# Back state of a three-step gated recurrence turned through DRAM instead of by TensorE, with the queues of all engines reordered around its hand-over

## The chip, the cores and the metric

The program runs on one core of a Trainium2 chip. The metric is device time in microseconds of one execution. It is bound to float32 accuracy, so every operand of a product is split into a high part and a low part (fp32r), and each product is three matmuls: high by high, high by low, low by high.

## The reference

For 32 graphs of 256 nodes with 256 features (`x`, shape 32 x 256 x 256, one shared `adj` of 256 x 256), four layers follow each other, each as `x = layernorm(x + layer(x))`:

```python
# layer 0: gated recurrence, 3 steps (both message directions use adj, so the two halves of w3, w4, w5 are summed)
for _ in range(3):
    a  = adj @ h
    z  = sigmoid(a @ W3 + h @ U3 + b)      # update gate
    r  = sigmoid(a @ W4 + h @ U3 + b)      # reset gate
    hv = tanh(a @ W5 + (r * h) @ U5 + b)
    h  = (1 - z) * h + z * hv
# layer 1: rel = adj.T * ((x Wq) @ (x Wk).T); rel = rel / row norm; out = rel @ (x Wv)
# layer 2: out = (adj @ x) @ W + b
# layer 3: out = norm_adj @ (x @ W) + b
```

## The kernel before

Two graphs form a pair; there are 16 pairs, and LAST is 15. The state of a pair is held in two forms. `feat` has features on the partitions and 512 nodes (two graphs) along the free axis; the products with U3 and with the reset state need it. `node` has nodes on the partitions; the product with adj (`mix`) needs it. After each step the new state comes out as `feat`, so it has to be turned to get `node`.

Two lanes work side by side, each with its own PSUM banks. The front lane does steps 0 and 1 of pair p; the back lane does step 2 of pair p-1 and then the other three layers (`main`) of that pair. At the end of step 1 the front lane writes the new state into the back lane's state (`hand_over_h`).

One step is, for each half k of the output features: `mix` (adj by node, 12 matmuls of 256 columns), `base` (U3 by feat), `reset`, `update`, `candidate_mixed` (a by W5) and `candidate_reset` (reset state by U5), each of the last five 6 matmuls of 512 columns. ScalarE (ACT) makes the high parts, the gates and tanh; VectorE (DVE) makes the low parts, the elementwise steps, the statistics of the layer norms, and the fills of PSUM with residual and bias; GpSimd (POOL) does the power -1/2 of the variances; SyncE (SP) issues the transfers.

Each engine runs its own instructions in a written order: `start()` (everything up to the first regular pair), `body(p, q)` in a loop over p = 2 to 14 with q = p - 1 (13 passes), and `finish()`. Every operation waits on semaphores by count and then does its work, so an operation that waits holds up everything behind it on its engine. The numbers of the loop body repeat with the period of one pass.

There were two ways to turn a state. The front state between step 0 and step 1 went through DRAM: VectorE transposes 32 x 32 blocks (`turn_state`, two instructions), SP writes them to a scratch tensor and reads them back with four transfers (`move_blocks`), ACT and VectorE split the result (`moved_hi`, `moved_lo`). The back state went through TensorE: `turn_h(state_b, ...)` issues four 128 x 128 transposes for each of two graphs into `front.ps1`, and `node_hi` and `node_lo` split from there. The next `mix(front, ...)` writes the same PSUM banks, so it waited for `state_b.s_node_lo`. In the loop the order on TensorE around it is: `mix_nodes(main, q, 1, 0..1)`, `convolve(main, q, 1, 0)`, the two `turn_h(state_b)`, `convolve(main, q, 1, 1)`, and in the next pass `mix(back)` twice, `mix(front)` twice, `base(back)` twice, `reset(back)`. There are 15 hand-overs: two in `start()`, 13 in the loop.

Of the kernel before, what the change touches and what calls it, by code (L numbers as in the profile page):

```python
# [21 lines left out]
P = 128  # L22
# [16 lines left out]
class State:  # L39


    def __init__(self, sb, sem, name, full, by_graph, by_blocks):
# [118 lines left out]
def build(nc, x, adj, w3_w, w3_b, u3_w, u3_b, w4_w, w4_b, w5_w, w5_b, u5_w, u5_b, wq, wk, wv,  # L161
          l2_w, l2_b, l3_w, l3_b, out):
    B, N, D = x.shape
# [12 lines left out]
    with ExitStack() as ctx:  # L176
# [43 lines left out]
        state_f = State(sb, sem, "hf", [P, C, T], [P, G, C, D], True)  # L220
        state_b = State(sb, sem, "hb", [P, C, T], [P, G, C, D], False)
# [14 lines left out]
        state_f.blocks, state_f.moved = quarters(front.gate), quarters(front.z)  # L236

# [6 lines left out]
        def nodes(name, dt=F32):  # L244
# [13 lines left out]
                      (nodes("v_hi", F32R), nodes("v_lo", F32R)), rel_split,  # L258
# [10 lines left out]
        main.sum_blocks, main.sum_moved = (t[:].rearrange("p g c d -> p (g c) d") for t in (main.normed, main.result))  # L269

# [56 lines left out]
        def _(sp):  # L327
# [72 lines left out]
            keep_input(0)  # L400
            with sp.Fori(1, LAST) as p:
# [4 lines left out]
                move_blocks(state_f, p)  # L406
                store(main, p - 1)
# [7 lines left out]
        def _(pool):  # L415
# [29 lines left out]
            def body(q):  # L445
# [3 lines left out]
                for k in range(2):  # L449
                    inverse_norm(main, q, k)  # L450
                for k in range(2):
                    inverse_std(main, q, 1, k)
# [5 lines left out]
            def finish():  # L458
# [7 lines left out]
                for k in range(2):  # L466
                    inverse_norm(last_pair, 0, k)
                inverse_std(last_pair, 0, 1, 0)
                inverse_norm(main, LAST - 1, 1)
                inverse_std(last_pair, 0, 1, 1)  # L470
                inverse_std(main, LAST - 1, 1, 1)
                inverse_std(main, LAST - 1, 2, 0)
                for k in range(2):
                    inverse_std(last_pair, 0, 2, k)
                inverse_std(main, LAST - 1, 2, 1)
                inverse_std(main, LAST - 1, 3, 0, True)
# [32 lines left out]
        def _(pe):  # L509
# [83 lines left out]
            def mix(L, n, k, pair=None, turned=False):  # L593
# [6 lines left out]
                if pair is not None and later(pair):  # L600
                    pe.wait_ge(state_b.s_node_lo, upto(pair - 1, k))
# [199 lines left out]
            def body(p, q):  # L801

                for k in range(2):
                    mix(back, q, k)
                for k in range(2):
                    mix(front, 2 * p, k, p)
                for k in range(2):
                    base(back, q, k)
                for k in range(2):
                    reset(back, q, k)  # L810
                candidate_mixed(back, q, 0)
                for k in range(2):
                    update(back, q, k)
                candidate_mixed(back, q, 1)
                for k in range(2):
                    candidate_reset(back, q, k)
                base(front, 2 * p, 0, p)
                reset(front, 2 * p, 0)
                base(front, 2 * p, 1, p)
                reset(front, 2 * p, 1)  # L820
                candidate_mixed(front, 2 * p, 1)
# [3 lines left out]
                update(front, 2 * p, 1)  # L825
                candidate_reset(front, 2 * p, 1)
                for k in range(2):
                    keys(main, q, k)
                values(main, q, 0)
                for k in range(2):  # L830
                    relate(main, q, k)
                base(front, 2 * p + 1, 0)
                values(main, q, 1)
                base(front, 2 * p + 1, 1)
                sum_squares(main, q, 0)
                attend(main, q, 0)
                sum_squares(main, q, 1)
                for k in range(2):
                    mix(front, 2 * p + 1, k)
                attend(main, q, 1)  # L840
                reset(front, 2 * p + 1, 0)
                candidate_mixed(front, 2 * p + 1, 0)
                reset(front, 2 * p + 1, 1)
                mix_nodes(main, q, 0, 0)
                update(front, 2 * p + 1, 0)
                mix_nodes(main, q, 0, 1)
                for k in range(2):
                    convolve(main, q, 0, k)
                candidate_reset(front, 2 * p + 1, 0)
                candidate_mixed(front, 2 * p + 1, 1)  # L850
                update(front, 2 * p + 1, 1)
# [3 lines left out]
                convolve(main, q, 1, 0)  # L855
                for k in range(2):
                    turn_h(state_b, p, k)
                convolve(main, q, 1, 1)

            def finish():  # L860

                mix(back, LAST - 1, 0)
                mix(front, 2 * LAST, 0, LAST)
                mix(back, LAST - 1, 1)
                mix(front, 2 * LAST, 1, LAST)
                for k in range(2):
                    base(back, LAST - 1, k)
                for k in range(2):
                    reset(back, LAST - 1, k)
                for k in range(2):  # L870
                    base(front, 2 * LAST, k, LAST)
                for k in range(2):
                    reset(front, 2 * LAST, k)
                candidate_mixed(front, 2 * LAST, 1)
                candidate_mixed(front, 2 * LAST, 0)
                update(front, 2 * LAST, 0)
                candidate_reset(front, 2 * LAST, 0)
                update(front, 2 * LAST, 1)
                candidate_reset(front, 2 * LAST, 1)
                update(back, LAST - 1, 0)  # L880
                candidate_mixed(back, LAST - 1, 0)
                for k in range(2):
                    turn_h(state_f, 2 * LAST + 1, k)
# [7 lines left out]
                candidate_reset(back, LAST - 1, 0)  # L891
                update(front, 2 * LAST + 1, 0)
                for k in range(2):
                    candidate_mixed(front, 2 * LAST + 1, k)
                candidate_reset(front, 2 * LAST + 1, 0)
                update(front, 2 * LAST + 1, 1)
                candidate_reset(front, 2 * LAST + 1, 1)
                candidate_mixed(back, LAST - 1, 1)
                candidate_reset(back, LAST - 1, 1)
                for k in range(2):  # L900
                    turn_h(state_f, 2 * LAST + 2, k)
                base(front, 2 * LAST + 2, 0)
# [7 lines left out]
                for k in range(2):  # L910
                    update(front, 2 * LAST + 2, k)
                candidate_mixed(front, 2 * LAST + 2, 0)
                candidate_reset(front, 2 * LAST + 2, 0)
                keys(main, LAST - 1, 0)
                candidate_mixed(front, 2 * LAST + 2, 1)
                candidate_reset(front, 2 * LAST + 2, 1)
                relate(main, LAST - 1, 0)
# [3 lines left out]
                values(main, LAST - 1, 0, True)  # L921
                keys(last_pair, 0, 0)
                relate(main, LAST - 1, 1)
                keys(last_pair, 0, 1)
                values(last_pair, 0, 0, True)
                for k in range(2):
                    relate(last_pair, 0, k)
                sum_squares(main, LAST - 1, 0)
# [1314 lines left out]
```

## Time and profile before

| | us |
|---|---|
| median of 3 runs | 1214.63 (1214.09 to 1214.99) |
| the profiled execution, its device time | 1214.77 |
| its span, first to last instruction | 1212.9 |
| TensorE busy in the span | 1198.3 |
| VectorE busy | 1002.6 |
| ScalarE busy | 655.7 |
| GpSimd busy | 191.7 |

The device time stands 1.9 us above the span: what lies before the first and after the last instruction. A matmul's duration in the trace is its latency; matmuls overlap, so what one costs TensorE is the distance from its start to the next start. Durations of other engines overlap their successor a little too. Starts are microseconds from the span's start.

### The profile page before, as it was taken

The numbers are of one execution on the slowest core, as the hardware profiler recorded it, in microseconds if no ns is written. First come the engines' busy times: TensorE is split into PE (matmuls) and PEld (weight loads), VectorE is DVE, ScalarE is ACT, GpSimd is POOL, SyncE is SP. The second block draws the span as 40 slices with busy tenths as digits, with TensorE's granted clock in tenths as the row PEclk, the third lists the DMA queues.
The fourth block names the chain that finished last, engine by engine and source line by source line (L and its number), as shares of the span: only waits on it lengthen the run. The fifth ranks groups of instructions, "written<-read, shape, count | busy, mean of one in ns | idle before, by whom it ended". The sixth has DMA issues, their size and how long they took to land.

```text
span 1212.9 us, 21243 instructions
## 1 busy us (share of the span) xinstructions
PE 1198.3 (99%) x7454; PEld 1079.2 (89%) x7454; DVE 1002.6 (83%) x2220; ACT 655.7 (54%) x1179; POOL 191.7 (16%) x447
## 2 busy tenths in 40 slices
PE   9999999999999999999999999999999999999997
PEld 8789899898988989899898998989889898998896
DVE  7689788897878879788897888978789797885898
ACT  5455555555555555555555555555555555554442
POOL 1002021110211203012020211102111030120022
PEclk9999999999999999999999999999999999999998
DMA  6030221303113030220302213031130302200001
GB/s 209 18 88 18 70 71 35 104 0 88 50 35 104 0 104 35 52 87 14 107 17 69 69 35 104 0 87 52 35 104 0 104 35 51 87 12 24 1 2 35
DMA packets 105021, 66.93 MB, mean 55 GB/s; under 512 B 65690, under 2 KB 98468, under 8 KB 104996
## 3 DMA queue, kind: packets, MB, share of 16 engines
q1 hardware_dynamic: 104784, 66.08, 18.2%
q0 software_dynamic: 192, 0.52, 0.2%
q8 instruction: 15, 0.25, 0.1%
q14 instruction: 10, 0.08, 0.0%
q10 hardware_dynamic: 20, 0.01, 0.0%
HBM read 35.13 MB, written 23.07 MB: 48 GB/s over the span
## 4 chain that ended last, share of the span: by engine, by line
PE 97%; DVE 2%; POOL 0%; ACT 0%; issue 0%; DVEq 0%; POOLq 0%
PE b_ps L520 41%; PE f_ps L520 32%; PE f_ps L515 15%; PE b_ps L515 7%; PE f_ps L682 1%; PE b_ps L746 1%; PE b_ps L564 0%; PE f_ps L1057 0%; DVE f_stats L1683 0%; DVE hf_feat L1699 0%; DVE f_gate L1699 0%; DVE b_rh_lo L1725 0%; PE b_ps L579 0%; DVE b_ps L1720 0%; PE f_ps L589 0%
## 5 line engine op out<-in xcount | busy, mean ns | idle before, releaser
L428 POOL TENSOR_TENSOR b_var_eps<-b_moments,eps 128x2 f32<-128x2 f32 x120 | 34.7, 289 | 904.2 <-DVE b_moments L1690 904.2
L1120 ACT ACTIVATE f_cand<-f_ps,bias_c 128x512 f32<-128x512 f32 x66 | 45.4, 689 | 85.2 <-PE f_ps L520 85.2
L430 POOL TENSOR_TENSOR b_rstd<-b_var_eps,neg_half 128x2 f32<-128x2 f32 x120 | 88.0, 733 | 9.4
L1068 ACT ACTIVATE b_rh_hi<-b_ps 128x512 fp32r<-128x512 f32 x90 | 53.6, 596 | 63.0 <-PE b_ps L520 62.9
L1108 ACT ACTIVATE f_gate<-f_ps,bias_r 128x512 f32<-128x512 f32 x66 | 45.3, 686 | 71.0 <-PE f_ps L520 71.0
L1068 ACT ACTIVATE b_a_hi<-normed 128x512 fp32r<-128x512 f32 x60 | 37.8, 630 | 60.0 <-DVE normed L1699 60.0
L520 PE MATMUL f_ps<-adjT_hi,hf_node_hi 128*128 128x256 f32 x264 | 66.4, 285 | 0.0
L520 PE MATMUL f_ps<-adjT_lo,hf_node_hi 128*128 128x256 f32 x264 | 65.0, 280 | 0.0
L1582 DVE TENSOR_TENSOR f_cand<-f_z,f_cand 128x512 f32<-128x512 f32 x66 | 45.4, 688 | 23.0 <-ACT f_cand L1120 22.9
L1725 DVE TENSOR_TENSOR b_rh_lo<-b_ps,b_rh_hi 128x512 fp32r<-128x512 f32 x90 | 61.1, 679 | 4.0 <-ACT b_rh_hi L1068 3.9
L1566 DVE TENSOR_TENSOR f_gate<-f_gate,hf_feat 128x512 f32<-128x512 f32 x66 | 44.7, 678 | 20.0 <-ACT f_gate L1108 20.0
L1068 ACT ACTIVATE f_a_hi<-f_ps 128x512 fp32r<-128x512 f32 x66 | 38.9, 591 | 38.3 <-PE f_ps L520 38.3
L1560 DVE TENSOR_TENSOR b_a_lo<-b_ps,b_a_hi 128x512 fp32r<-128x512 f32 x30 | 19.4, 686 | 48.6 <-ACT b_a_hi L1068 48.6
L1116 ACT ACTIVATE f_z<-f_ps,bias_z 128x512 f32<-128x512 f32 x66 | 45.0, 683 | 26.6 <-PE f_ps L515 26.5
L1560 DVE TENSOR_TENSOR f_a_lo<-f_ps,f_a_hi 128x512 fp32r<-128x512 f32 x66 | 44.9, 681 | 13.8 <-ACT f_a_hi L1068 13.6
L1187 ACT ACTIVATE result<-result,b_shift,b_rstd 128x256 f32<-128x256 f32 x56 | 30.6, 594 | 46.2 <-POOL b_shift L436 46.2
L520 PE MATMUL f_ps<-hf_feat_hi,u3T_hi 128*128 128x512 f32 x132 | 52.3, 396 | 0.2 <-DVE u3T_lo L1486 0.2
L1068 ACT ACTIVATE hf_feat_hi<-hf_feat 128x512 fp32r<-128x512 f32 x64 | 38.7, 627 | 25.1 <-DVE hf_feat L1646 22.3
L520 PE MATMUL f_ps<-f_a_hi,w4T_hi 128*128 128x512 f32 x132 | 51.9, 393 | 0.0
L520 PE MATMUL f_ps<-hf_feat_hi,u3T_lo 128*128 128x512 f32 x132 | 51.7, 391 | 0.0
L515 PE MATMUL f_ps<-f_a_lo,w34T_hi 128*128 128x512 f32 x132 | 51.5, 390 | 0.0
L520 PE MATMUL f_ps<-f_rh_hi,u5T_lo 128*128 128x512 f32 x132 | 51.5, 390 | 0.0
(340 smaller groups left out, 4304.4 us busy)
## 6 DMA issues: line engine op xcount, KB each, us to landing
x_front<-in_x SPq DMA_DIRECT2D x16, 512.0 KB, 3.9
x_blocks<-in_x SPq DMA_DIRECT2D x60, 128.0 KB, 2.9
input_t<-hf_feat SPq DMA_DIRECT2D x15, 512.0 KB, 3.0
turn_sum<-normed SPq DMA_DIRECT2D x14, 512.0 KB, 2.7
result<-turn_sum SPq DMA_DIRECT2D x56, 128.0 KB, 2.9
turn_f<-f_gate SPq DMA_DIRECT2D x14, 512.0 KB, 2.7
f_z<-turn_f SPq DMA_DIRECT2D x56, 128.0 KB, 2.8
out<-result SPq DMA_DIRECT2D x14, 512.0 KB, 3.2
```

The source lines that it names most:

```text
L428: pool.tensor_tensor(Y.var_eps[:, g], Y.moments[:, g, :, 1], eps[:], ALU.add).then_inc(Y.s_var, 1)
L430: pool.tensor_tensor(Y.rstd[:, g], Y.var_eps[:, g], neg_half[:], ALU.pow).then_inc(Y.s_rstd, 1)
L515: last = pe.matmul(bank, s, m, start=start and i == 0, stop=stop and i == len(terms) - 1, skip_group_check=True)
L520: return pe.matmul(bank, s, m, start=start, stop=stop, skip_group_check=True)
L1068: return act.activation(dst, src, ACT.Copy)
L1108: act.activation(L.gate[:, k], L.ps0[:, k], ACT.Sigmoid, bias=bias_r[:, k:k + 1]).then_inc(L.s_r, 1)
L1116: act.activation(L.z[:, k], L.ps0[:, k], ACT.Sigmoid, bias=bias_z[:, k:k + 1]).then_inc(L.s_z, 1)
L1120: act.activation(L.cand[:, k], L.ps1[:, k], ACT.Tanh, bias=bias_c[:, k:k + 1]).then_inc(L.s_tanh, 1)
L1560: dve.tensor_tensor(L.a_lo[:, k], L.ps1[:, k], full(L.a_hi[:, k]), ALU.subtract).then_inc(L.s_a_lo, 1)
L1566: dve.tensor_tensor(L.gate[:, k], L.gate[:, k], L.state.feat[:, k], ALU.mult).then_inc(L.s_rh, 1)
L1582: dve.tensor_tensor(L.cand[:, k], L.z[:, k], L.cand[:, k], ALU.mult).then_inc(L.s_zc, 1)
L1725: dve.tensor_tensor(lo[:, g], src, full(hi[:, g]), ALU.subtract).then_inc(done, 1)
```

## The change

The back state is turned the way the front state already was. `State` always has the semaphores of the block path; the back state gets a DRAM scratch, its blocks are written into the back lane's `kept` tile and read back into its `cand` tile. SP moves the back's blocks behind the front's in each pass, ahead of the store. All of `turn_h(state_b, ...)`, `node_hi(state_b, ...)` and `node_lo(state_b, ...)` go; two `turn_state`, two `moved_hi` and two `moved_lo` per pair come in. `mix(front, ...)` no longer waits for the back's `node_lo`, but for the tanh that last read its bank. The tiles of `x_hi`, `x_lo` and of the attention's `v_hi`, `v_lo` are swapped: v now shares the back lane's `a` tiles, x has its own. The order of all queues is written anew.

```diff
@@ set-up
+        state_b.scratch = scratch("turn_b")
+        state_b.blocks, state_b.moved = quarters(back.kept), quarters(back.cand)
...
-                      (nodes("v_hi", F32R), nodes("v_lo", F32R)), rel_split,
+                      (per_graph(back.a_hi), per_graph(back.a_lo)), rel_split,
...
+        main.x_hi, main.x_lo = nodes("x_hi", F32R), nodes("x_lo", F32R)
@@ SyncE
+            move_blocks(state_b, 1)
             with sp.Fori(1, LAST) as p:
...
                 move_blocks(state_f, p)
+                move_blocks(state_b, p + 1)
                 store(main, p - 1)
@@ TensorE, mix
-                if pair is not None and later(pair):
-                    pe.wait_ge(state_b.s_node_lo, upto(pair - 1, k))
+                if pair is not None:
+                    pe.wait_ge(front.s_tanh, upto(n - 1, k))
@@ TensorE, body, first operations (was: mix back x2, mix front x2, base back x2, reset back x2, ...)
                 for k in range(2):
+                    mix(front, 2 * p, k, p)
+                for k in range(2):
+                    base(back, q, k)
+                base(front, 2 * p, 0, p)
+                for k in range(2):
                     mix(back, q, k)
+                reset(front, 2 * p, 0)
...
@@ TensorE, body, last operations
                 for k in range(2):
                     mix_nodes(main, q, 1, k)
-                convolve(main, q, 1, 0)
-                for k in range(2):
-                    turn_h(state_b, p, k)
-                convolve(main, q, 1, 1)
+                for k in range(2):
+                    convolve(main, q, 1, k)
@@ ScalarE, body, first operations
                 for k in range(2):
+                    input_hi(p, k)
+                for k in range(2):
+                    moved_hi(state_b, q, k, q + 1)
+                for k in range(2):
+                    a_hi(front, 2 * p, k)
+                for k in range(2):
                     a_hi(back, q, k)
@@ VectorE, body, first operations
                 for k in range(2):
+                    turn_blocks(p, k)
+                for k in range(2):
+                    input_lo(p, k)
+                for k in range(2):
+                    moved_lo(state_b, q, k)
@@ VectorE, body, last operations
                 hand_over_h(p, 0)
+                keep(front, 2 * p + 1, 1)
                 conv_x_lo(main, q, 1, 1)
-                fill(main, q, 1, 0)
+                turn_state(state_b, p, 0)
                 candidate_part(front, 2 * p + 1, 1)
-                keep(front, 2 * p + 1, 1)
+                hand_over_h(p, 1)
                 conv_ax_lo(main, q, 1, 0)
-                hand_over_h(p, 1)
+                turn_state(state_b, p, 1)
                 fill(main, q, 1, 1)
                 conv_ax_lo(main, q, 1, 1)
...
@@ TensorE, start, around the first hand-over
-                base(back, 0, 0)
-                for k in range(2):
-                    turn_h(state_b, 0, k)
-                base(back, 0, 1)
+                for k in range(2):
+                    mix(front, 2, k, 1)
+                prepare(8)
+                candidate_mixed(front, 2, 1)
+                for k in range(2):
+                    base(back, 0, k)
                 for k in range(2):
                     mix(back, 0, k)
```

In `finish()` the last pair has no hand-over; its order changes as well, with the same operations.

## Rows read from the trace of the kernel before

**Rows 1.** The page: busy us of each engine, share of the span, instructions.

```profile
PE 1198.3 (99%) x7454; PEld 1079.2 (89%) x7454; DVE 1002.6 (83%) x2220; ACT 655.7 (54%) x1179; POOL 191.7 (16%) x447
```

**Rows 2.** The page: the chain that ended last, share of the span by engine.

```profile
PE 97%; DVE 2%; POOL 0%; ACT 0%; issue 0%; DVEq 0%; POOLq 0%
```

**Rows 3.** Waits of TensorE: waiter, what released it, us in total, times, longest.

```profile
PE b_ps L520 <- ACT hb_feat_hi L1068: 2.3, 2, 1.4
```

**Rows 4.** Windows (length, busy by engine, clock): start; 13 passes; finish; one pass; its end.

```profile
0.00:124.55 124.55, 120.25 (x707) 106.11 (x708) 97.97 (x200) 67.97 (x117) 14.46 (x35) 1.00 0.27 81
124.55:1082.47 957.92, 957.92 (x5983) 864.37 (x5981) 799.78 (x1768) 530.76 (x962) 154.71 (x364) 1.00 0.19 57
1082.47:1205.63 123.16, 120.13 (x770) 108.67 (x768) 100.17 (x237) 57.01 (x102) 19.60 (x42) 0.99 0.03 10
566.66:640.35 73.69, 73.69 (x463) 66.49 (x461) 61.58 (x136) 40.87 (x76) 11.89 (x28) 1.00 0.19 57
617.00:640.35 23.35, 23.35 (x157) 21.38 (x156) 21.87 (x51) 12.17 (x22) 3.34 (x6) 1.00 0.00 0
```

**Rows 5.** TensorE around a hand-over, in time: start, duration, what.

```profile
560.18 0.28 PE L520 MATMUL b_ps<-norm_adjT_hi,b_a_hi 128*128 128x256 f32 x1
...
564.38 1.03 PE L682 MATMUL f_ps<-ident,hb_feat 128*128 128x128 f32 x8
...
566.66 0.28 PE L520 MATMUL b_ps<-adjT_hi,hb_node_hi 128*128 128x256 f32 x1
...
569.46 0.28 PE L520 MATMUL f_ps<-adjT_hi,hf_node_hi 128*128 128x256 f32 x1
...
577.72 0.39 PE L515 MATMUL b_ps<-b_a_hi,w5T_hi 128*128 128x512 f32 x1
...
579.08 0.39 PE L515 MATMUL b_ps<-b_a_hi,w34T_hi 128*128 128x512 f32 x1
```

**Rows 6.** TensorE where it goes from 256-column matmuls to 512 and back.

```profile
532.86 0.40 PE L520 MATMUL f_ps<-hf_feat_hi,u3T_hi 128*128 128x512 f32 x1
...
534.26 0.28 PE L520 MATMUL b_ps<-wvT_hi,sum_hi 128*128 128x256 f32 x1
```

**Rows 7.** VectorE around the hand-over and at an earlier turn of the front state.

```profile
528.75 0.70 DVE L1626 STREAM_TRANSPOSE f_gate<-hf_feat 128x512 f32<-128x512 f32 x1
...
561.47 0.69 DVE L1582 TENSOR_TENSOR f_cand<-f_z,f_cand 128x512 f32<-128x512 f32 x1
...
563.27 0.68 DVE L1588 TENSOR_TENSOR hb_feat<-f_cand,f_kept 128x512 f32<-128x512 f32 x1
563.87 0.69 DVE L1720 TENSOR_TENSOR b_ps<-normed,bias_out 128x512 f32<-128x512 f32 x1
...
570.82 0.15 DVE L1690 BATCH_NORM_AGGREGATE b_moments<-b_stats 128x2 f32<-128x6 f32 x1
```

**Rows 8.** ScalarE: tanh before the hand-over; last normalisation of the pair.

```profile
560.38 0.69 ACT L1120 ACTIVATE f_cand<-f_ps,bias_c 128x512 f32<-128x512 f32 x1 [0.15 <-PE f_ps L520]
...
572.66 1.09 ACT L1187 ACTIVATE result<-result,b_shift,b_rstd 128x256 f32<-128x256 f32 x2 [0.25 <-POOL b_shift L436]
```

**Rows 9.** SyncE's queue: the front's blocks written and read back; x_blocks loaded.

```profile
529.48 0.34 SPq L375 DMA_DIRECT2D turn_f<-f_gate  x1
532.16 1.73 SPq L378 DMA_DIRECT2D f_z<-turn_f  x4
...
584.21 3.05 SPq L356 DMA_DIRECT2D x_blocks<-in_x  x4
```

**Rows 10.** The tile turn_f: issue to landing of its read-backs.

```profile
DMA to landing us min/median/max: 2.5/2.8/3.1
```

**Rows 11.** The page: a 512 KB load from DRAM, us from issue to landing.

```profile
x_front<-in_x SPq DMA_DIRECT2D x16, 512.0 KB, 3.9
```

**Rows 12.** TensorE in start, around the first hand-over.

```profile
46.56 0.61 PE L520 MATMUL f_ps<-f_rh_lo,u5T_hi 128*128 128x512 f32 x2
...
53.46 0.28 PE L520 MATMUL b_ps<-adjT_hi,hb_node_hi 128*128 128x256 f32 x1
```

More of the change, by code:

```diff
@@ L1034, in start @@
                 for k in range(2):
-                    mix(front, 3, k)
+                    reset(front, 3, k)
+                candidate_mixed(front, 3, 0)
                 mix_nodes(main, 0, 0, 0)
-                for k in range(2):
-                    reset(front, 3, k)
-                convolve(main, 0, 0, 0)
                 update(front, 3, 0)
                 mix_nodes(main, 0, 0, 1)
+                for k in range(2):
+                    convolve(main, 0, 0, k)
                 update(front, 3, 1)
-                convolve(main, 0, 0, 1)
-                candidate_mixed(front, 3, 0)
                 candidate_reset(front, 3, 0)
@@ L1281, in finish @@
[L1281 to L1292 removed]
+                    feat_hi(state_f, 2 * LAST + 1, k)
@@ L1832, in body @@
                 moments_of(main, q, 1, 1)
+                a_lo(front, 2 * p + 1, 1)
                 fill(main, q, 0, 0)
+                conv_ax_lo(main, q, 0, 0)
+                normalise(main, q, 1, 1)
                 reset_h(front, 2 * p + 1, 0)
-                normalise(main, q, 1, 1)
+                stats_of(main, q, 2, 0)
+                conv_x_lo(main, q, 0, 1)
+                fill(main, q, 0, 1)
+                moments_of(main, q, 2, 0)
+                input_nodes_lo(p + 1, 0)
@@ L1895, in finish @@
                 node_lo(state_f, 2 * LAST + 1, 0)
+                for k in range(2):
+                    reset_h(back, LAST - 1, k)
+                node_lo(state_f, 2 * LAST + 1, 1)
                 feat_lo(state_f, 2 * LAST + 1, 0)
-                node_lo(state_f, 2 * LAST + 1, 1)
+                a_lo(front, 2 * LAST + 1, 0)
                 feat_lo(state_f, 2 * LAST + 1, 1)
-                rh_lo(back, LAST - 1, 1)
+                a_lo(front, 2 * LAST + 1, 1)
+                for k in range(2):
+                    rh_lo(back, LAST - 1, k)
@@ L1918, in finish @@
+                feat_lo(state_f, 2 * LAST + 2, 0)
+                node_lo(state_f, 2 * LAST + 2, 0)
                 feat_lo(state_f, 2 * LAST + 2, 1)
[L1919 removed]
+                candidate_part(back, LAST - 1, 0)
+                node_lo(state_f, 2 * LAST + 2, 1)
                 candidate_part(back, LAST - 1, 1)
[L1921 to L1923 removed]
@@ L2110, in start @@
+                scale_columns()
+                a_lo(front, 2, 1)
+                feat_lo(state_b, 0, 0)
+                prep_lo(8)
+                prep_lo(9)
+                turn_blocks(1, 0)
+                feat_lo(state_b, 0, 1)
+                for k in range(2):
+                    moved_lo(state_b, 0, k)
                 for k in range(2):
                     a_lo(back, 0, k)
-                for k in range(2):
-                    reset_h(back, 0, k)
+                reset_h(back, 0, 0)
```

923 lines of the change are left out of this document (442 added, 481 removed).

## Prediction

> **What bounds the kernel now.** I read the page first: TensorE is busy 1198.3 of 1212.9 us, VectorE 1002.6 [rows 1]. The chain that ended last is TensorE for 97% [rows 2]. The waits of TensorE say where the other 14.6 us are: its longest wait, 2.3 us, is for the high part of the back state in the start [rows 3]. The stretches say the rest: in the 13 passes of the loop TensorE is busy for all 957.92 us at a granted clock of 1.00, the 2.4 GHz level, so one pass is 73.69 us of work without a gap; finish has 123.16 us with 120.13 busy [rows 4]. Two things follow. Work taken off TensorE in a pass is gained whole, if nothing else then ends later than TensorE. And VectorE is the engine that could: 61.58 us of a pass of 73.69, and 21.87 of the last 23.35 us, where the hand-over lies [rows 4].
>
> **What is removed.** The turn of two graphs is eight transposes. They begin at 564.38, the 12 matmuls of the second convolve follow, and the next pass begins at 566.66, 2.28 us later [rows 5]. Two `mix` of 12 such matmuls take 569.46 - 566.66 = 2.80, so 1.40 each [rows 5]. The eight transposes cost 2.28 - 1.40 = 0.88 us, 0.11 each. Times 15 hand-overs: 13.2 us.
>
> A rule weighed here: the Trainium skill ("TensorE: Matmul & The Clock Gate", Part 4: PE-mode transpose) gives about 275 ns for a 128 x 128 transpose inside a kernel, mostly access latency. By that the 120 transposes would be worth 33 us. The trace agrees with 275 as a latency, but eight together lasted 1.03 us [rows 5]; they overlap, so the sum goes by 0.88.
>
> **What is added on VectorE and ScalarE.** Two block transposes of 0.70 us [rows 7] per pair. Independent VectorE instructions start 0.60 apart (563.27 to 563.87, [rows 7]), a dependent one some 0.7 to 0.8 after its source. `moved_hi`, `moved_lo` take the place of `node_hi`, `node_lo` with the same 128 x 512 elements; I count them equal. So VectorE gets 61.6 + 1.3 = 62.9 us in a pass of about 72.8: 86% instead of 84%. It still isn't the bound by its sum; the question is the order at single places.
>
> **The hand-over, step by step.** New times count from T, the end of `candidate_reset(front, 2p+1, 1)` on TensorE (before: 560.18, [rows 5]). In the new order TensorE does two `mix_nodes` and two `convolve`, 4 x 1.40, so the pass ends at T + 5.6. An instruction that needs a matmul's result starts 0.2 us after the last one issued: tanh at 560.38, 0.69 long [rows 8]. Then on VectorE: candidate_part at T + 0.9, hand_over at 1.7, conv_ax_lo at 2.35, the second turn_state at 2.95, fill at 3.6, written at 4.3.
>
> First narrow place: `convolve(main, q, 1, 1)` needs that fill. Before, the fill ended at 563.87 + 0.69 = T + 4.4 [rows 7], and the transposes on TensorE covered it (convolve began at T + 5.1: 566.66 less 1.40). Now convolve could begin at T + 4.2 and finds the fill at 4.3. Cost 0.1 us a pass; bounds 0 (all VectorE steps 0.1 earlier) and 0.6 (one more instruction slips before the fill).
>
> Second: the way through DRAM. The front's last block transpose ends at 528.75 + 0.70 = 529.45 [rows 7]; the write is issued at 529.48, the first read-back at 532.16, four read-backs in 1.73 us [rows 9], so the last about 1.3 after the first, each landing after 2.8 (2.5 to 3.1) [rows 10]. That is 0.03 + 2.68 + 1.3 + 2.8 = 6.8 us. The back's last block transpose ends at T + 3.65, its data are there at T + 10.45. With B = T + 5.6 for the start of the next pass: B + 4.85.
>
> TensorE's new order gives this cover: mix(front) twice 2.80, base(back) twice and base(front, 0), three times 1.36 (577.72 to 579.08, [rows 5]), so mix(back, 0) is due at B + 6.9. ScalarE before it: the last statistics end about B + 1.9, the last normalise_rows starts 1.7 later (570.82 + 0.15 to 572.66, [rows 7, 8]) and takes 1.1, then input_hi twice to B + 5.6, then moved_hi twice to B + 6.7. The first moved_hi is due before B + 6.9 and the second one before B + 7.35 (the first graph's high part is 4 x 2 matmuls, a third of which remain). So the data have about 0.8 us to spare before ScalarE even asks and nearly 0.3 more before TensorE does. Cost 0, bounds 0 and, by an x_front load's landing of 3.9 us [rows 11] in place of the write's 2.68, 0.2.
>
> Third: base(front, 0) is due at B + 5.5 and now stands behind normalise_rows and input_hi on ScalarE (its second half ready at 5.6, due at 6.0) and input_lo on VectorE (ready 6.3, due 6.65). Cost 0, 0.3 to spare.
>
> On SP the move of the back blocks stands ahead of the store and the next loads. The store is ready at about B + 4.7, the read-backs are issued by T + 3.65 + 4.4 = B + 2.5, so nothing behind waits longer than before. DRAM traffic is no bound: DMA's share in a pass is 0.19 [rows 4].
>
> I walked the rest of the pass in the same way (0.60 a VectorE instruction, 0.2 + 0.6 to 0.7 a ScalarE one): every operand is ready before TensorE asks, most by 0.3 to 2 us. Such a walk is good to some 0.3 us.
>
> **Order.** A 512-column product behind 256-column ones takes 1.40 (532.86 to 534.26, [rows 6]) instead of 1.36. The new pass has 8 such changes against 5 or 6 before: +0.1 a pass at most; I take 0.06.
>
> **Start and finish.** At the first hand-over TensorE now has to cover nearly the whole way. Z is the end of the product at 46.56, 0.45 later: 47.0. Before, mix(back) began at 53.46 [rows 12] = Z + 6.45, of which 2.72 were products, 0.88 transposes, 2.85 idle. New: blocks ready Z + 3.1, data Z + 9.9, one moved_hi, mix(back) at about Z + 10.55. Between stand mix(front) twice, candidate_mixed and base(back) twice, 6.9 us, and one small prepare of 0.4; idle 3.2. Two waits of 0.15 and 0.3 behind it (second moved_hi; a_lo with no cover before reset). So here the 0.88 are gone into idle time: +0.9 back, bounds -0.3 and +2. The other hand-over of the start saves its 0.88. Finish has the same products, all dependent chains of two pairs, and 3 us of idle time either way [rows 4]; its reordering and that of the first 20 us I take at -0.5, bounds -3 and +3.
>
> **Sum**, against the profiled execution's 1214.77: -13.2 +0.9 +13 x 0.1 +13 x 0.06 -0.5 = -10.7, so 1204.1. The median of the runs lies 0.14 lower than the profiled one: 1204.0.
>
> **Rivals.**
> A. VectorE slips. For: 21.87 of 23.35 us busy at the end of a pass [rows 4], and the walk leaves 0.1 to 0.5 us at many places there. If 0.5 us a pass come out at TensorE (most of one 0.60 step): 13 x 0.4 more than forecast, 1209. Against: at the start of a pass VectorE has free time, so slips don't add up from pass to pass.
> B. The other side, slower: the state arrives late. Place: mix(back, 0) in each pass, where TensorE stands in order behind it. It decides when the data come more than 1.1 us late by my walk, and outweighs the gain of 0.7 a pass above 1.8. The nearest rows: four 128 KB loads took 3.05 us to issue instead of 1.73 [rows 9], and 3.9 instead of 2.68 for the first transfer [rows 11]: 2.5 us late, 1.4 of wait a pass, 13 x 1.4 = 18: 1222. Against: the front's and the sum's turn ran with the short times in every pass. The Trainium skill ("VectorE: DVE Perf Modes", The three transpose paths) warns that a plain strided DMA used for a transpose is far slower than other ways. Here DMA moves whole rows and VectorE does the element turn; the read-backs landed in 2.5 to 3.1 us [rows 10], so the trace doesn't bear the rule out for this form.
> C. More than forecast: the new order also takes the 3 us of waiting out of finish and the first hand-over costs nothing: 1214.6 - 13.2 - 3 + 0.8 = 1199.
> D. The clock: if longer waits in start lowered the granted clock, more is lost; with the waits that start had before it stayed at 1.00, and the only lower value, 0.99, is in finish [rows 4]. Within the bounds above.
>
> **Numbers.** Forecast 0.67 (own range 1201 to 1207), A 0.15, B 0.07, C 0.11. The time is the forecast's, 1204. The range 1200 to 1209 leaves out B, a third of A and half of C, some 0.17. A measurement here can't tell less than 0.2%, 2.4 us, from no change. Faster by more than that (below 1212.2): the forecast, C and most of A, 0.90; the same 0.04, the tail of A; slower 0.06, B.
>
> **What would show it.** Right: passes of 72.9 us (72.8 to 73.2) with TensorE's wait in them under 0.3; no transposes of hb_feat; the back's read-backs landed before moved_hi asks; a 3 us wait before the first mix(back). Wrong: passes above 73.3; a wait of mix(back) for moved_hi or of ScalarE for a DMA (B); waits of convolve for a fill or of the products for lows (A); passes without any wait and yet longer, which would mean that the transposes cost less than 0.88.

## The result and the profile after

The changed kernel takes 1219.57 us (median of 6 runs, 1219.05 to 1220.7), the kernel before beside it 1214.81 (1213.44 to 1216.31): a ratio of 1.004, interval 1.0027 to 1.0053. It is slower by 0.4%. I had forecast 1204.0 with a range of 1200 to 1209, and gave "slower" 6 in 100.

The page of the changed kernel: TensorE, and the chain that ended last. Beside [rows 1, 2] TensorE has 120 instructions less, but only 3.3 us less busy time, and the chain, 97% TensorE before, now goes through VectorE and GpSimd.

```profile
PE 1195.0 (98%) x7334; PEld 1063.9 (87%) x7334; DVE 1030.5 (85%) x2250; ACT 665.0 (55%) x1179; POOL 217.8 (18%) x447
...
PE 84%; DVE 6%; POOL 4%; issue 2%; ACT 2%; DMA 1%; ACTq 0%; SPq 0%; POOLq 0%; DVEq 0%
```

Windows of the changed kernel: start, the 13 passes, finish up to the span's end, and one pass. As in [rows 4], each line has the length, the busy time of TensorE, its weight loads, VectorE, ScalarE and GpSimd, then the granted clock, the DMA share and GB/s.

```profile
0.00:127.04 127.04, 120.77 (x691) 104.81 (x692) 100.56 (x204) 67.61 (x116) 14.19 (x35) 1.00 0.31 92
127.04:1087.60 960.56, 955.34 (x5878) 852.21 (x5877) 825.41 (x1794) 540.39 (x962) 178.06 (x364) 1.00 0.24 71
1087.60:1217.90 130.30, 118.92 (x770) 106.90 (x768) 104.53 (x254) 57.04 (x101) 25.50 (x48) 0.98 0.06 21
570.36:644.27 73.91, 73.52 (x455) 65.55 (x453) 63.50 (x139) 41.56 (x74) 13.70 (x28) 1.00 0.24 71
```

A pass is 960.56 / 13 = 73.89 us instead of 73.69 [rows 4]: 2.6 us more in 13 passes. Start is 127.04 instead of 124.55, 2.5 more. Finish to the span's end is 130.30 against 1212.9 - 1082.47 = 130.43. Together the 5.0 us by which the span grew. The clock is the same in the passes (1.00), so rival D has no part.

The longest entry of TensorE's waits in the changed kernel (waiter, releaser, us in total, times, longest) is new:

```profile
PE f_ps L525 <- ACT hf_feat_hi L1067: 5.6, 14, 0.4
```

That is my "third narrow place", the one that I had priced at nothing. The names in it: `turn_blocks` on VectorE makes `hf_feat` from the loaded `x_blocks`, `input_hi` on ScalarE and `input_lo` on VectorE split it into `hf_feat_hi` and `hf_feat_lo`, and `base(front, 0)` on TensorE reads these. `feat_lo` on VectorE makes `hb_feat_lo` for `base(back)`. `normalise_rows(main, q, 3, k)` is the last normalisation of the pair behind; only the store needs its result. TensorE in time:

```profile
568.31 0.63 PE L525 MATMUL b_ps<-w3s_hi,b_rh_lo 128*128 128x256 f32 x4
568.85 0.39 PE L525 MATMUL b_ps<-w3s_hi,b_rh_hi 128*128 128x256 f32 x1
...
570.36 0.28 PE L525 MATMUL f_ps<-adjT_hi,hf_node_hi 128*128 128x256 f32 x1
...
573.16 0.39 PE L525 MATMUL b_ps<-hb_feat_hi,u3T_hi 128*128 128x512 f32 x1
...
576.48 0.47 PE L525 MATMUL f_ps<-hf_feat_hi,u3T_hi 128*128 128x512 f32 x1 [0.39 <-ACT hf_feat_hi L1067]
...
578.06 0.28 PE L525 MATMUL b_ps<-adjT_hi,hb_node_hi 128*128 128x256 f32 x1
```

The pass begins at B = 570.36. The two base(back) keep TensorE for 2.77 us from 573.16, so base(front, 0) is due at 575.93. It begins at 576.48, 0.55 late, and then takes 578.06 - 576.48 = 1.58 instead of 1.36, as its low parts are late too: 0.77 us a pass. Only 0.39 of it stands in brackets as idle; the rest shows as longer "busy" rows. The first row pair shows a smaller loss: four matmuls of 0.12 take from 568.31 to 568.85, and the next begins only when the fill of convolve(1, 1) has ended (568.13 + 0.67 = 568.80 on VectorE). The pair of convolve takes 2.98, not 2.80.

ScalarE at that place:

```profile
572.92 1.10 ACT L1186 ACTIVATE result<-result,b_shift,b_rstd 128x256 f32<-128x256 f32 x2 [1.76 <-POOL b_shift L441]
574.73 1.09 ACT L1186 ACTIVATE result<-result,b_shift,b_rstd 128x256 f32<-128x256 f32 x2 [0.71 <-POOL b_shift L441]
575.73 1.14 ACT L1067 ACTIVATE hf_feat_hi<-hf_feat 128x512 fp32r<-128x512 f32 x2
576.77 1.14 ACT L1067 ACTIVATE hb_node_hi<-b_cand 128x512 fp32r<-128x512 f32 x2
```

VectorE, and below it GpSimd:

```profile
572.11 0.15 DVE L1689 BATCH_NORM_AGGREGATE b_moments<-b_stats 128x2 f32<-128x6 f32 x1
572.17 1.26 DVE L1613 TENSOR_TENSOR hb_feat_lo<-hb_feat,hb_feat_hi 128x512 fp32r<-128x512 f32 x2
573.36 1.29 DVE L1645 STREAM_TRANSPOSE hf_feat<-x_blocks 128x512 f32<-128x512 f32 x2
```

```profile
572.37 0.52 POOL L441 TENSOR_TENSOR b_shift<-b_neg_mean,b_rstd 128x2 f32<-128x2 f32 x1
572.84 0.65 POOL L433 TENSOR_TENSOR b_var_eps<-b_moments,eps 128x2 f32<-128x2 f32 x1
573.57 0.69 POOL L435 TENSOR_TENSOR b_rstd<-b_var_eps,neg_half 128x2 f32<-128x2 f32 x1
574.22 0.20 POOL L438 TENSOR_TENSOR b_neg_mean<-b_moments,neg_one 128x2 f32<-128x2 f32 x1
574.50 0.20 POOL L441 TENSOR_TENSOR b_shift<-b_neg_mean,b_rstd 128x2 f32<-128x2 f32 x1
```

In these rows input_hi's source, the block transposes, is there from 573.36 + 0.69 on, 1.7 us before ScalarE turns to it. ScalarE stands at normalise_rows(3, 1), which waits for the shift of 574.50. From the end of the moments to that start it is 574.73 - 572.26 = 2.47 us; I had copied 1.7 from the kernel before [rows 7, 8]. There VectorE is idle next to the second half of GpSimd's chain, and the same var_eps takes 0.20 us. First GpSimd, then VectorE, of the kernel before:

```profile
571.23 0.20 POOL L428 TENSOR_TENSOR b_var_eps<-b_moments,eps 128x2 f32<-128x2 f32 x1
```

```profile
574.26 1.29 DVE L1560 TENSOR_TENSOR b_a_lo<-b_ps,b_a_hi 128x512 fp32r<-128x512 f32 x2 [3.29 <-ACT b_a_hi L1068]
```

The way through DRAM was not late: on SyncE's queue the read-backs are issued 2.7 us after the write, from 0.5 us into the pass, and moved_hi (576.77) waits for nothing.

```profile
568.23 0.34 SPq L378 DMA_DIRECT2D turn_b<-b_kept  x1
570.89 1.73 SPq L381 DMA_DIRECT2D b_cand<-turn_b  x4
```

Start: TensorE at its end. Both turn_states stand ahead of conv_ax_lo(1, 0) on VectorE, and TensorE waits for its low part (b_rh_lo):

```profile
122.87 0.36 PE L525 MATMUL b_ps<-w3s_hi,b_rh_hi 128*128 128x256 f32 x1 [0.29 <-ACT b_rh_hi L1067]
...
124.85 0.73 PE L525 MATMUL b_ps<-w3s_hi,b_rh_lo 128*128 128x256 f32 x4 [0.80 <-DVE b_rh_lo L1724]
```

### The profile page after: what moved, and what is told of

Its sections match the earlier page's. It is cut to its first block, busy times and chain, and to the rows that moved or that the text cites. A ratio compares the mean times of both kernels' runs of the same rounds, so it can differ in the third digit from the quotient of the medians.

```text
span 1217.9 us, 21096 instructions
## 1 busy us (share of the span) xinstructions
PE 1195.0 (98%) x7334; PEld 1063.9 (87%) x7334; DVE 1030.5 (85%) x2250; ACT 665.0 (55%) x1179; POOL 217.8 (18%) x447
## 4 chain that ended last, share of the span: by engine, by line
PE 84%; DVE 6%; POOL 4%; issue 2%; ACT 2%; DMA 1%; ACTq 0%; SPq 0%; POOLq 0%; DVEq 0%
PE b_ps L525 35%; PE f_ps L525 27%; PE f_ps L520 14%; PE b_ps L520 7%; POOL b_rstd L435 2%; POOL b_var_eps L433 1%; DVE b_stats L1682 1%; PE b_ps L751 1%; POOL b_shift L441 1%; ACT hf_feat_hi L1067 1%; ACT result L1067 1%; DMA b_cand<-turn_b 1%; DMA turn_b<-b_kept 0%; DVE b_rh_lo L1724 0%; DVE normed L1698 0%
## 5 line engine op out<-in xcount | busy, mean ns | idle before, releaser
L433 POOL TENSOR_TENSOR b_var_eps<-b_moments,eps 128x2 f32<-128x2 f32 x120 | 51.5, 429 | 892.4 <-DVE b_moments L1689 892.4
L435 POOL TENSOR_TENSOR b_rstd<-b_var_eps,neg_half 128x2 f32<-128x2 f32 x120 | 98.7, 822 | 9.4
L1067 ACT ACTIVATE x_hi<-normed 128x512 fp32r<-128x512 f32 x60 | 37.8, 630 | 46.4 <-DVE normed L1698 46.4
L1613 DVE TENSOR_TENSOR hf_feat_lo<-hf_feat,hf_feat_hi 128x512 fp32r<-128x512 f32 x64 | 42.3, 679 | 24.6 <-ACT hf_feat_hi L1067 24.6
L1565 DVE TENSOR_TENSOR b_gate<-b_gate,hb_feat 128x512 f32<-128x512 f32 x30 | 20.7, 692 | 38.8 <-ACT b_gate L1107 38.8
L520 PE MATMUL f_ps<-f_a_hi,w5T_hi 128*128 128x512 f32 x132 | 51.7, 392 | 1.8 <-DVE f_a_lo L1559 1.8
L520 PE MATMUL f_ps<-f_a_hi,w34T_hi 128*128 128x512 f32 x132 | 51.8, 392 | 0.0
L525 PE MATMUL f_ps<-f_a_hi,w4T_lo 128*128 128x512 f32 x132 | 51.7, 392 | 0.0
L520 PE MATMUL f_ps<-f_a_lo,w5T_hi 128*128 128x512 f32 x132 | 51.6, 391 | 0.0
```

The source lines that it names most:

```text
L433: pool.tensor_tensor(Y.var_eps[:, g], Y.moments[:, g, :, 1], eps[:], ALU.add).then_inc(Y.s_var, 1)
L435: pool.tensor_tensor(Y.rstd[:, g], Y.var_eps[:, g], neg_half[:], ALU.pow).then_inc(Y.s_rstd, 1)
L520: last = pe.matmul(bank, s, m, start=start and i == 0, stop=stop and i == len(terms) - 1, skip_group_check=True)
L525: return pe.matmul(bank, s, m, start=start, stop=stop, skip_group_check=True)
L1067: return act.activation(dst, src, ACT.Copy)
L1565: dve.tensor_tensor(L.gate[:, k], L.gate[:, k], L.state.feat[:, k], ALU.mult).then_inc(L.s_rh, 1)
```

## Experiments

Theory Q (queue): the whole loss of 0.77 us is ScalarE's order, in which normalise_rows(3), waiting for GpSimd, stands ahead of input_hi. Rivals: D, the state comes late through DRAM; V, VectorE is overloaded; and that the transposes were worth little. Later runs add C (contention between VectorE and GpSimd) and L (what waits behind moved_hi in ScalarE's queue). These letters are not those of the prediction: its rival B is D here, and its D was the clock. Every ratio is to the kernel before on the same chip; the change itself has 1.0040.

**1. normalise_rows(3) behind moved_hi** (ScalarE; start and finish likewise)

```diff
 input_hi(p, k); moved_hi(state_b, q, k, q + 1)
+for k in range(2):
+    normalise_rows(main, q - 1, 3, k)
 a_hi(front, 2 * p, k)
 ...
-for k in range(2):
-    normalise_rows(main, q, 3, k)      # end of the pass
```

> Theory Q (queue of ScalarE): normalise_rows(3) of the pair before, which waits for GpSimd's shift, stands ahead of input_hi, and this alone holds base(front, 0) for 0.77 us in a pass. With both normalise_rows moved behind moved_hi, input_hi runs as soon as its block transpose is there (573.36 + 0.69 in the profiled pass, due 575.93), so base(front, 0) starts without a wait: passes of 73.1 us instead of 73.89, 13 x 0.77 = 10 us less than the changed kernel, some 1209.5. Theory D (the state comes late through DRAM): the wait only moves to mix(back), passes stay near 73.9, 1219. Theory V (VectorE overloaded): the low parts come no sooner, passes stay above 73.6, 1216 or more.

Measured: 1210.31 us, ratio 0.9962 (0.9949 to 0.9976). This one move gives 9.3 us, 13 x 0.71, and the change is now faster than the kernel before. ScalarE, a pass that begins at 565.74: input_hi runs 3.7 us into it, and the wait for hf_feat_hi is gone from TensorE's waits. Below it the window of the passes, without an idle moment, 951.17 / 13 = 73.17 each.

```profile
569.47 1.23 ACT L1067 ACTIVATE hf_feat_hi<-hf_feat 128x512 fp32r<-128x512 f32 x2 [2.93 <-DVE hf_feat L1645]
570.60 1.14 ACT L1067 ACTIVATE hb_node_hi<-b_cand 128x512 fp32r<-128x512 f32 x2
571.64 2.07 ACT L1186 ACTIVATE result<-result,b_shift,b_rstd 128x256 f32<-128x256 f32 x4
573.61 1.06 ACT L1067 ACTIVATE f_a_hi<-f_ps 128x512 fp32r<-128x512 f32 x2
```

```profile
126.61:1077.78 951.17, 951.17 (x5878) 853.47 (x5877) 825.33 (x1795) 538.68 (x962) 177.92 (x364) 1.00 0.24 72
```

VectorE's busy time is what it was in the change (825.4), so V falls: the engine was not overloaded.

**2 and 3. GpSimd delayed, with each order**

```diff
 pool.wait_ge(Y.s_var, ln(q, j, g))
+if j == 3 and not ending:
+    pool.tensor_tensor(spare[:, g], Y.var_eps[:, g], neg_half[:], ALU.pow)
 pool.tensor_tensor(Y.rstd[:, g], ...)
```

> The changed kernel with one more GpSimd operation (0.69 us, its result is not used) ahead of the rstd of each j = 3 statistics. Theory Q: normalise_rows(3, 1) starts two such operations later (1.4 us), input_hi with it, and TensorE pays nearly all: 13 x 1.4 = 18 us more, 1238; at least 13 x 0.7 = 9 more if only one of the two counts. Theories D and V: GpSimd's shift is on no path, 1219.5 as without it.

> The same extra GpSimd operation in the kernel with normalise_rows(3) behind moved_hi. Theory Q: GpSimd's result is asked for some 4 us later there, so the delay costs nothing: within 1 us of the kernel without the delay (1209.5). Theories D and V expect no cost here either, but at 1216 to 1219; what tells them apart is the pair with and without the move.

Measured: in the change 1230.46 us (ratio 1.0127, 1.0111 to 1.0142), 10.9 more, 0.84 a pass; with normalise_rows moved 1209.44 (0.9954, 0.994 to 0.9967), nothing more. So GpSimd's chain is on the path in the one order and not in the other: Q. TensorE's wait for hf_feat_hi in the first grows from 5.6 to 17.5 us:

```profile
PE f_ps L528 <- ACT hf_feat_hi L1070: 17.5, 14, 1.3
```

I had put 1.4 a pass. Two extra operations start 0.66 later each, 1.3 in all; but the delay moves GpSimd's second var_eps out of VectorE's way, and in the same trace it takes 0.19 instead of 0.65, which leaves 0.84:

```profile
577.65 0.19 POOL L434 TENSOR_TENSOR b_var_eps<-b_moments,eps 128x2 f32<-128x2 f32 x1
```

**4. The transposes twice, in the kernel before**

```diff
 pe.wait_ge(S.s_feat, upto(v))
+if S is state_b:
+    for c in range(C):
+        for k in range(C):
+            pe.transpose(front.ps1[:, g, ...], S.feat[:, k, ...], ident[:])
 turn(front.ps1, g, S.feat, S.s_turned)
```

> The kernel before with the eight TensorE transposes of the back state issued twice. If the transposes are worth what I took for them, 0.88 us a hand-over, 15 hand-overs cost 15 x 0.88 = 13.2 us: 1228. The rival, that they lie beside other work or overlap and are worth much less, so that there was little to gain: 1217 or less. By 275 ns each, not overlapping, it would be 33 us, 1248.

Measured: 1228.89 us, ratio 1.0116 (1.01 to 1.0131): 13.65 more, 0.91 a hand-over. The price of the removed work was right. TensorE, sixteen transposes from 1092.15 to 1093.82, 1.67 us; in the kernel before, eight from 564.38 [rows 5] to the row below them, 0.79. The convolve behind takes 1.49 instead of 1.40 (565.17 to 566.66), so the 0.88 of the prediction is 0.79 of transposes and 0.09 of a slower start behind them, and doubling adds 1.67 - 0.79 = 0.88 in a pass.

```profile
1092.15 0.60 PE L691 MATMUL f_ps<-ident,hb_feat 128*128 128x128 f32 x4
...
1093.82 0.37 PE L520 MATMUL b_ps<-w3s_hi,b_rh_hi 128*128 128x256 f32 x1
```

```profile
565.17 0.37 PE L520 MATMUL b_ps<-w3s_hi,b_rh_hi 128*128 128x256 f32 x1
```

**5. Why GpSimd's shift came late: feat_lo(state_b) behind turn_blocks**

```diff
 turn_blocks(p, k)
+for k in range(2):
+    feat_lo(state_b, q, k)
 ...
-for k in range(2):
-    feat_lo(state_b, p, k)      # end of the pass before
```

> The changed kernel with VectorE's feat_lo(state_b) of both halves behind turn_blocks of the next pass. Question: why does ScalarE get GpSimd's shift so late? Theory C (contention): GpSimd's small operations take 0.52 to 0.65 us instead of 0.20 when VectorE runs a 128x512 operation with two inputs in SBUF beside them; beside block transposes (one input) they take 0.20. Then the var_eps and shift at 572 to 573 take 0.20 each, normalise_rows(3, 1) starts 0.45 us earlier after its moments, and TensorE's wait for hf_feat_hi falls from 0.39 to near 0; against that stands a new wait of base(back) for the low parts, which end 0.3 us after they are due. Sum: 1217 to 1220. The rival (GpSimd's times don't depend on VectorE): the times stay 0.5 to 0.65, the wait for hf_feat_hi stays, and the new wait is added: 1223.

Measured: 1221.71 us, ratio 1.0059 (1.0046 to 1.0073). GpSimd in the changed order:

```profile
572.62 0.20 POOL L441 TENSOR_TENSOR b_shift<-b_neg_mean,b_rstd 128x2 f32<-128x2 f32 x1
572.77 0.19 POOL L433 TENSOR_TENSOR b_var_eps<-b_moments,eps 128x2 f32<-128x2 f32 x1
```

The shift takes 0.20 instead of 0.52, with VectorE idle beside it, and var_eps 0.19 instead of 0.65, as the block transposes begin: it is contention. From the end of the moments (572.37 + 0.15) to normalise_rows(3, 1) it is 1.7 us again, as in the kernel before:

```profile
574.20 1.09 ACT L1186 ACTIVATE result<-result,b_shift,b_rstd 128x256 f32<-128x256 f32 x2 [0.25 <-POOL b_shift L441]
```

The Trainium skill ("SBUF — State Buffer", Who interferes with whom) states that a VectorE instruction with two SBUF inputs contends with a GpSimd instruction that reads SBUF, and calls the shared port pair an exclusive lock. The trace agrees: var_eps ended at 573.49 in the change, just after the feat_lo that ran beside it (572.17 + 1.26 = 573.43). With the 0.78 us back, input_hi starts 4.59 us into the pass instead of 5.37, and the wait for hf_feat_hi is gone. But base(back) now waits for the low parts, and the pair takes 3.72 us instead of 2.77, more than I had put. The time lies between my two numbers and is no gain:

```profile
PE b_ps L525 <- DVE hb_feat_lo L1613: 4.4, 14, 0.4
```

**6. The fill ahead of the second turn_state**, on top of 1

```diff
+fill(main, q, 1, 1)
 turn_state(state_b, p, 1)
-fill(main, q, 1, 1)
```

> normalise_rows(3) behind moved_hi, and in VectorE's order the fill of convolve(1, 1) ahead of the second turn_state(state_b). The two convolve take 2.98 us instead of 2.80 in the changed kernel; if the fill is what they wait for, 13 x 0.18 = 2.3 us less than without this (1210.3): 1208.0. The blocks for the DRAM way come 0.6 later, which the slack there (theory Q: 1.4 us) covers. Theory D would have that move cost 13 x 0.6 = 8 us instead: 1216.

Measured: 1218.66 us, ratio 1.0031 (1.0019 to 1.0044): 8.3 slower than without, where I expected 2.3 faster. It is nearer to theory D's 1216 than to my 1208, and 2.7 above even that, though run 1 had excluded D for the change. TensorE's longest wait in the sum, and ScalarE in a pass that begins at 570.43:

```profile
PE f_ps L525 <- DVE f_a_lo L1559: 6.5, 12, 0.6
```

```profile
576.29 1.15 ACT L1067 ACTIVATE hb_node_hi<-b_cand 128x512 fp32r<-128x512 f32 x2 [0.72 <-DMA b_cand<-turn_b]
577.35 2.06 ACT L1186 ACTIVATE result<-result,b_shift,b_rstd 128x256 f32<-128x256 f32 x4
579.32 1.06 ACT L1067 ACTIVATE f_a_hi<-f_ps 128x512 fp32r<-128x512 f32 x2
```

The state comes 5.9 us into the pass. That is in time for mix(back), which begins at its due time. But behind the waiting moved_hi stood 2.06 us of normalise_rows, where I had just put them, and behind these a_hi(front): its low part is late for reset(front, 0), which takes 2.31 us instead of 1.38. This is theory L: the wait is paid by what is queued behind it. Also mix(front) took 2.93 instead of 2.80 here: its low part, which VectorE makes behind the first statistics, is ready 1.13 us into the pass (570.90 + 0.66) instead of 0.95.

**7. The blocks written to DRAM twice**, on top of 1: the slack of the way

```diff
+if S is state_b:
+    sp.wait_ge(S.s_written, 32 * turn - 16)
+    sp.dma_start(S.scratch..., S.blocks).then_inc(S.s_written, 16)
```

> normalise_rows(3) behind moved_hi, and the blocks of the back state written to DRAM twice, one after the other, so that the read-backs land about 2.7 us later. It measures the slack of the way through DRAM. I read 1.4 us of slack for the first read (landed some 4.75 us into the pass, due at 6.2 for ScalarE's copy): then each pass waits 1.3 us, 13 x 1.3 = 17 us more than 1210.3: 1227. With the 1.1 us of slack of my prediction: 13 x 1.6 = 21, 1231. If the way had been late already: 13 x 2.7 = 35, 1245. If it were hidden by 3 us or more: 1210.

Measured: 1251.47 us, ratio 1.0296 (1.0282 to 1.031): 41 more, where I had put 17 to 21, or 35 with the way late already. The passes take 36 of it, 987.39 / 13 = 75.95 against 73.17, 2.8 each, for a delay of 2.67; the rest lies mainly in start. That is the whole delay, though the way had slack, so something beyond the late data costs here. The queue behind moved_hi can be that, and the second wait of TensorE is where it would show:

```profile
PE b_ps L528 <- ACT hb_node_hi L1070: 19.9, 14, 2.9
PE f_ps L528 <- DVE f_a_lo L1562: 10.0, 12, 0.9
```

```profile
131.72:1119.11 987.39, 960.31 (x5878) 854.11 (x5877) 826.35 (x1795) 538.12 (x962) 178.21 (x364) 1.00 0.25 76
```

(The 3.15 a pass in the expectation of run 10 is all of the 41 us divided by 13; a pass itself shows 2.8.)

**8. Run 6 with the start mended**: on VectorE conv_x_lo, conv_ax_lo and fill ahead of the turn_states that held them, and base(front, 2, 0) on TensorE moved into the wait of the first hand-over, with what feeds it.

> The kernel of the fill ahead of turn_state, with the start mended too: at its end conv_x_lo, conv_ax_lo(1, 0) and fill(1, 1) stand ahead of the turn_states that they waited for (TensorE lost 0.6 + 1.3 us there), and base(front, 2, 0) is moved into the wait for the first hand-over, with input_hi and input_lo ahead of it (1.36 us). Expected: 1.9 + 1.4 = 3.3 us less than without these edits, 1204.7; if the first hand-over is bound by the way through DRAM alone and base(front, 2, 0) fits in no gap, 1206.

Measured: 1218.28 us, ratio 1.0031 (1.0019 to 1.0043). The passes had the fault of run 6. The loop began at 124.95 us instead of 127.87, but the medians differ by 0.4 only. The spans differ by 1.9 (1216.4 and 1218.3): the profiled execution of run 6 was one of its longer ones, with 3.8 us of waiting for the first state from DRAM in start, where run 1 had 2.8. So it does not measure the start well; run 12 does it again.

**9 and 10. a_hi(front) ahead of normalise_rows**, with one write and with two

```diff
 moved_hi(state_b, q, k, q + 1)
-for k in range(2):
-    normalise_rows(main, q - 1, 3, k)
 a_hi(front, 2 * p, k)
-for k in range(2):
-    a_hi(back, q, k)
+normalise_rows(main, q - 1, 3, 0)
+a_hi(back, q, 0)
+normalise_rows(main, q - 1, 3, 1)
+a_hi(back, q, 1)
```

> As the kernel with normalise_rows(3) behind moved_hi, but with ScalarE's a_hi(front) of both halves, then the first a_hi(back), ahead of them. Theory L (what lies behind the DRAM way on ScalarE): moved_hi waits for the DRAM way, and 2.07 us of normalise_rows and a_hi(front) queue behind it, so that VectorE's a_lo and TensorE's reset(front, 0) were met with only 0.5 us to spare. Where the state is in time, as here, the order costs and gains nothing: 1210.3, passes of 73.1 us.

> The same with the back state's blocks written to DRAM twice. With normalise_rows ahead of a_hi(front) the second write cost 41 us, 3.15 a pass, more than its own 2.7. Theory L: half of it was the queue behind moved_hi. With a_hi(front) ahead, what is left is the wait of mix(back) itself, 1.3 to 1.6 us a pass: 1227 to 1231. Theory D (the DRAM way has no slack and its delay is paid whole, whatever stands behind it): 13 x 2.7 to 3.15 = 35 to 41 us: 1245 to 1251.

Measured: 1209.34 us (0.9951, 0.9937 to 0.9964) and 1237.61 (1.0182, 1.0168 to 1.0195). With one write the order changes nothing, as expected. The second write costs 28.3 us here and 41.2 with the other order; the result lies between L's 1227 to 1231 and D's 1245 to 1251. TensorE waits for hb_node_hi as long as in run 7 (19.9 us in all), and its wait for f_a_lo, 10.0 there, is gone: L holds in that some third of the 41 was the queue. My 1.3 to 1.6 a pass was too low: a pass is 1.91 longer (74.97 against 73.06), 24.8 us in 13. The rest lies mainly in start and has the clock in it. At the end of a wait of 2.9 to 3.0 us of TensorE for the first state from DRAM, or within 1 us of it, its granted clock fell to 0.50, the 1.2 GHz level, for 3.4 us in run 10 and 6.8 us in run 7, and in both for 3.4 us more behind a wait of 1.7 to 1.8 us in the second pass. This fall is the prediction's rival D; in the change, where the waits are shorter, start has 1.00. The middle passes, at 1.00 in both runs, still differ by 0.9: 2.8 against 1.9 for the second write. First ScalarE, then TensorE, of a pass that begins at 582.03:

```profile
589.67 1.15 ACT L1070 ACTIVATE hb_node_hi<-b_cand 128x512 fp32r<-128x512 f32 x2 [2.68 <-DMA b_cand<-turn_b]
```

```profile
590.44 0.36 PE L528 MATMUL b_ps<-adjT_hi,hb_node_hi 128*128 128x256 f32 x1 [1.35 <-ACT hb_node_hi L1070]
```

The data are there at 7.64, so 4.97 with one write, against 4.85 forecast; mix(back) begins 8.41 into the pass instead of 6.9, 1.5 late, and it and the reset behind it take another 0.4. The slack of mix(back) is then 2.67 - 1.5 = 1.2 us; I had said 1.1.

**11. The fill ahead of turn_state, with a_hi(front) ahead of normalise_rows**, and input_nodes_lo(p + 1, 1) ahead of the statistics

```diff
+fill(main, q, 1, 1)
 turn_state(state_b, p, 1)
-fill(main, q, 1, 1)
 conv_ax_lo(main, q, 1, 1)
+input_nodes_lo(p + 1, 1)
 stats_of(main, q, 3, 0)
```

> The same order on ScalarE (one write), and on VectorE fill(1, 1) ahead of the second turn_state(state_b), and input_nodes_lo(p + 1, 1) ahead of the statistics. With the fill alone and normalise_rows ahead of a_hi(front), the way through DRAM came 1.0 us later and cost 8.3 us. Theory L: with a_hi(front) first the later state is in time for mix(back) (5.8 us into the pass, due at 6.4), reset(front, 0) waits for nothing, and convolve and mix(front) take 2.80 each: passes of 72.95 us, 1208. Theory D: it costs as before, 1218.

Measured: 1207.46 us, ratio 0.9934 (0.9921 to 0.9948). What cost 8.3 us in run 6 gains 1.9 here, together with the move of input_nodes_lo, which no run takes alone; mix(front) is back at 2.80 and reset(front, 0) at 1.39. ScalarE waits for the DRAM way as long as there (0.72), and nobody pays, as only the copy of 1.07 us stands ahead of what is urgent. The passes are 948.41 / 13 = 72.95 us.

```profile
570.65 1.15 ACT L1067 ACTIVATE hb_node_hi<-b_cand 128x512 fp32r<-128x512 f32 x2 [0.72 <-DMA b_cand<-turn_b]
571.71 1.07 ACT L1067 ACTIVATE f_a_hi<-f_ps 128x512 fp32r<-128x512 f32 x2
```

**12. Run 11 with the start of run 8**

> That kernel with the start mended as in the earlier run (there the loop began at 124.95 us instead of 127.87, 2.9 us sooner, though the passes were long). Theory L: 1208 less 2 to 3 us, 1205 to 1206, below both the kernel before and the change by 0.7 to 1.1%. Theory D: 1215.

Measured: 1205.95 us (1205.32 to 1206.96), ratio 0.9924 (0.991 to 0.9938): faster than the kernel before by 0.8%, than the change by some 1.1%. Windows of start, passes, finish:

```profile
0.00:125.07 125.07, 120.48 (x691) 104.22 (x691) 100.52 (x203) 67.88 (x116) 14.16 (x35) 1.00 0.30 90
125.07:1073.69 948.62, 948.62 (x5879) 852.88 (x5877) 827.01 (x1795) 538.00 (x962) 174.46 (x364) 1.00 0.24 72
1073.69:1204.10 130.41, 119.07 (x770) 106.91 (x768) 104.61 (x254) 56.95 (x101) 25.20 (x48) 0.99 0.07 23
```

## Why the prediction was wrong

- "Third: [...] Cost 0, 0.3 to spare" is the step that failed. It costs 13 x 0.77 = 10.0 us, and run 1 gave 9.3 of it back. The walk had the right queue and the right due time, but gave normalise_rows(3, 1) the start "1.7 later" of the kernel before. It is 2.47 later: next to the second half of GpSimd's chain VectorE was idle then and now runs feat_lo (run 5: 0.20 instead of 0.52 and 0.65, and 1.7 again). A duration was carried over without what ran beside it. With that 0.78 more, input_hi ends 6.5 into the pass, 0.5 late, not 0.4 early; and input_lo 7.3, 0.65 late, not 0.35 early.
- The price of the transposes, 0.88, was right: run 4 has 0.88 in the pass and 0.91 by the medians. The reading "0.11 each" was not: they come 0.10 apart, and 0.09 of the 0.88 is the slower convolve behind them.
- "First narrow place", the fill: forecast 0.1, measured 0.18, 1 us over 13 passes. It can be had back only if the queue behind moved_hi is in order (runs 6, 11).
- The order switches: run 11's pass has neither of the two waits and is 72.95 us. With 73.69 - 0.88 = 72.81 that leaves 0.14 for them, where I took 0.06 and called 0.1 the most: another 1 us. It is a remainder, not measured alone. Passes in all: 73.89 - 72.97 = 0.92 more than forecast, 12.0 us.
- "Second", the DRAM way: cost 0 was right, data at 4.97 instead of 4.85, slack 1.2 instead of 1.1 (run 10). Rival B did not happen in the change. What I priced in it was only TensorE's wait; the queue on ScalarE behind moved_hi is as near to the edge (runs 6, 7).
- Start: forecast some 1.1 less (two hand-overs of 0.88, less 0.9, and half of the 0.5), measured 2.5 more, so 3.6 us off. At its end the turn_states stand ahead of conv_ax_lo: the last two mix_nodes and two convolve take 3.44 and 4.09 instead of 2.80 each, 1.9 in all. At the first hand-over mix(back) begins at 58.41, where I had 57.55: Z was 47.49, not 47.0, and the way from it took 10.9, not 10.55. Run 12, which mends both places, has 2.0 back. Finish: as forecast within 0.5.
- Sum: 12.0 + 3.6 = 15.6 of the 15.7 us by which forecast and profiled span differ.
- Rival A named a slip at VectorE of 0.4 a pass. The place was ScalarE behind GpSimd and the size 0.77, so none of my cases was this one. What the prediction named as a sign of being wrong (passes above 73.3) did come. With 0.3 to spare in a walk good to "some 0.3 us", 6 in 100 for slower was too little.

What stays open: the 0.8 us in start that lie in neither of its two places, as no run takes the first hand-over alone, and what the mended start is worth to better than a microsecond (0.4 and 1.5 by the medians of runs 8 and 12, 1.9 and 1.9 by their spans).

## What to carry to other kernels

In an in-order queue, price each wait by what stands behind it: a side result that waits for a slow chain (here the last normalisation) belongs behind the copies that the bounding engine is due to read, and the copy that waits for a transfer has only urgent work behind it. When work is taken off the bounding engine, the margins of all its operands shrink by as much, so a time of the old trace may be carried over only with what ran beside it. A walk whose margins are as small as its error is a forecast for both signs.

## What the runs showed of the hardware

- A GpSimd add or multiply on 128x2 elements takes 0.20 us, and 0.52 to 0.65 beside a 128x512 VectorE operation with two SBUF inputs; beside block transposes it stays at 0.20 (the change at 574.22, run 5).
- TensorE transposes of 128 x 128 in a row come 0.10 us apart: eight take 0.79, sixteen 1.67, and the 256-column product behind them takes 0.09 longer (the kernel before, run 4).
- A 512 KB write to DRAM in the middle of the hand-over delays the read-backs by 2.67 us; its price was 1.9 or 2.8 us a pass, by ScalarE's order alone (runs 10, 7).
- Where TensorE waited 2.9 to 3.0 us for the first state, in a stretch where it was busy 5.6 to 5.8 of 10 us, the granted clock fell from 1.00 to 0.50 for 6.8 and 3.4 us (runs 7, 10, around 60 us).
- x_front landed in 4.8 us instead of 3.9 [rows 11], at a place where nothing waited for it. Its load now has the x_blocks loads 0.5 us behind it (before: 9.3 us); whether this or the added traffic slows it was not tested.
